# Input loaded group by group among the weights, shorter stores and loads of the far sets, and the heads' first stacks issued ahead of their tables

## The chip, the cores and the metric

The program runs on one core of a Trainium2 chip. The metric is the device time of one execution in microseconds (us). The core has five engines that run their own instruction streams: PE (TensorE; "PEld" are its weight loads), DVE (VectorE), ACT (ScalarE), POOL (GpSimd) and SP (SyncE, which here only issues DMAs). DMAs are moved by 16 shared DMA engines.

## What is computed

The reference is a network of eight residual stages on x of 4 x 1024 x 256 in float32. The change touches the first stage and the start of the program:

```python
x = x + _L0_attn_a_ref(_layernorm(x, axis=-1), W_q, W_k, W_v, W_o, W_down_kv, W_up_k, W_up_v)

# _L0_attn_a_ref, with 16 heads of 16
q = x @ W_q
latent_kv = (x @ W_k + x @ W_v) @ W_down_kv      # 64 wide
k_rec, v_rec = latent_kv @ W_up_k, latent_kv @ W_up_v
scores = einsum('bhqd,bhkd->bhqk', q, k_rec) / sqrt(256)
scores = scores * exp(-0.01 * |i - j|)
attn = softmax(scores); out = attn @ v_rec; return out @ W_o
```

Seven further stages follow (a mixture of experts, a retention, the experts again, a windowed attention, a low-rank FFN, a gated recurrence, the FFN again). The change does not touch their code.

## The kernel before

X, the residual stream, stays in SBUF as one tile of 128 partitions x 32 tiles of tokens x 256. A group is four of these tiles, 512 tokens; there are NG = 8 groups, two to each of the 4 batches (h = 0 and h = 1). `network` opens a first block in which SP loads `ident` (64 KB), groups 0 and 1 of X (1 MB) and the other six (3 MB), and waits for the first two. The other engines wait at the end of that block. Then stage A (`attention_decay`) runs in three phases, each with a barrier behind it.

**Projection** (`project_latent`, names `s0Ap_`). SP starts with `ph.start`, which adds a constant to each of the phase's 19 counting semaphores, loads six weights and then two tables (`falls`, `grows`, each one row of decay repeated on 128 partitions, 512 KB). DVE waits for all six weights (line 1586), adds WkT and WvT, makes the LayerNorm of group 0, copies out the product with W_down_kv (`wlat`, line 1590), and makes the LayerNorm of group 1. PE waits for all weights too, forms `wlat`'s product (line 1639), and only then transposes group 0 (line 132). From there each group g passes through the same turn: PE multiplies the latent (L1649) and q (L1656), transposes group g + 1, and multiplies k (L1665) and v (L1671); DVE multiplies each of q and k by both tables, which gives four sets F (0: q by falls, 1: q by grows, 2: k by grows, 3: k by falls; L1602); ACT rounds each set to its top part (L1500), and DVE (sets 0 and 1, L1505) or POOL (sets 2 and 3, L1511) forms the rest. SP stores top and rest of each set to the DRAM tensor `parts`: 64 stores of 512 KB in all, 8 to a group, in rows of 2 KB.

**Heads** (`heads_decay`, names `s0Ah_`). Two heads make a pair, and a pair has 16 turns (8 key tiles x 2 heads). SP loads for each pair two stacks, `plus` (sets 0 and 2) and `minus` (sets 1 and 3, the far side of the diagonal), each by 8 DMAs. At the phase's start SP issues in this order: `table` and `seen`, the first plus stack, then, once POOL has written `ones`, twelve DMAs of `ones` into rows of the six k tiles, and then the second plus, first minus and third plus stacks. PE waits for the twelve and for a zeroed PSUM bank before anything else, then computes 30 score turns ahead (`score`, two matmuls of 128 x 512 each, L2055), of which DVE takes the maximum (L2000) with the help of `table`, out of two PSUM buffers. Then the main loop runs: next to each further score turn PE forms the shifted scores (L2080), a transposed diagonal tile (L2089) and, after ACT's exponential (L2024), the product with V (L2100). The rows of `ones` are read from L2080 on. The minus stack is only multiplied where the key tile lies after the query tile, so key tile 0 and query tile 7 of it are never read.

**Output** (`project_heads`, names `s0Ao_`) follows; it does not change.

The lines that matter most:

```python
pe.wait_ge(weights, loaded)            # projection, PE and DVE: all six weights
pe.wait_ge(oned, 16 * 12)              # heads, PE, before the first score
```

## Time and profile before

| | us |
|---|---|
| median of 3 runs | 3270.99 (3268.53 to 3271.00) |
| the profiled execution | 3270.93 |
| its span, first to last record | 3269.2 |
| until the first matmul of the groups (L1649) | 27.6 |
| last bytes of `parts` stored | 134 |
| first matmul of the heads (L2055) | 150.4 |
| first matmul of their main loop (L2080) | 188.8 |

Over the span PE is busy for 86%, DVE for 60%, ACT for 48%, POOL for 31%. The page's slices show PE nearly full in the heads and in most later stages, and idle or light in the first 150 us. The granted TensorE clock has two levels, 1.2 GHz (0.50 in the rows) and 2.4 GHz (1.00). A row of the timeline gives start, busy time, engine, line, what is written from what, and in brackets how long the engine sat idle before it and what ended that.

### The profile page before, as it was taken

To read this page: it belongs to the slowest core of one execution; us is meant where nothing else is said; L and a number is where in the kernel's file an instruction comes from. 1 tells how busy PE (TensorE), PEld (TensorE's weight loads), DVE (VectorE), ACT (ScalarE), POOL (GpSimd) and SP (SyncE) were. 2 spreads that over 40 slices of the span, in tenths; PEclk is the share of its full clock that TensorE was granted. 3 is DMA by queue.
4 is the path that set the end of the run, shared out by engine and by line. 5 is a ranking of instruction groups with operands and counts; after the bars stand their busy time and mean duration, and the time that the engine had idled before them with its cause. 6 is when DMAs were issued, how large, how long until landed. Compare 5 with 4: busy or idle time off the path is not lost. (4 is left out here: it accounts for less than half of the span.)

```text
span 3269.2 us, 48231 instructions
## 1 busy us (share of the span) xinstructions
PE 2802.9 (86%) x15883; PEld 1690.3 (52%) x15883; DVE 1958.6 (60%) x4266; ACT 1558.7 (48%) x2949; POOL 1004.0 (31%) x1384
## 2 busy tenths in 40 slices
PE   6599999999986299997883499996969997888879
PEld 3244444444443198985551498983534443534443
DVE  6578878888826744443558644444956663527852
ACT  3347777777751145453111345442326665245544
POOL 3322222222201145452001245442664442120112
PEclk9779999999998599998996699997979998898879
DMA  7813232323224144432003244423243442200001
GB/s 254 282 46 83 66 86 67 85 67 80 62 70 134 45 91 86 95 71 65 0 0 130 65 96 84 98 38 89 79 123 96 101 99 66 56 1 0 0 7 46
DMA packets 183271, 253.89 MB, mean 78 GB/s; under 512 B 39416, under 2 KB 124152, under 8 KB 183056
## 3 DMA queue, kind: packets, MB, share of 16 engines
q1 hardware_dynamic: 151616, 216.89, 22.3%
q0 software_dynamic: 30720, 33.98, 6.5%
q8 instruction: 113, 1.85, 0.2%
q14 instruction: 102, 0.84, 0.1%
q10 hardware_dynamic: 720, 0.33, 0.1%
HBM read 156.53 MB, written 93.00 MB: 76 GB/s over the span
## 5 line engine op out<-in xcount | busy, mean ns | idle before, releaser
L2000 DVE CUSTOM_DVE_ANT_0 s0Ah_SD<-s0Ah_ps_s,s0Ah_table 128x1024 f32<-128x1024 f32 x512 | 607.1, 1223 | 157.1 <-PE s0Ah_ps_s L2055 157.1
L2024 ACT ACTIVATE s0Ah_PM<-s0Ah_ps_x 128x512 f32<-128x512 f32 x1024 | 530.1, 601 | 188.0 <-PE s0Ah_ps_x L2080 98.1
L2055 PE MATMUL s0Ah_ps_s<-s0Ah_plus_k,s0Ah_plus_q 48*128 48x512 f32 x1024 | 422.9, 477 | 31.9 <-DMA s0Ah_minus_k<-s0Ah_ones 28.0
L1980 POOL TENSOR_TENSOR s0Ah_DG<-s0Ah_SD,s0Ah_mx 128x128 f32<-128x128 f32 x512 | 205.5, 401 | 554.0 <-DVE s0Ah_mx L2000 554.0
L2055 PEld LDWEIGHTS s0Ah_ps_s<-s0Ah_plus_k,s0Ah_plus_q 48*128 48x128 f32 x1024 | 167.4, 193 | 279.6 <-DVE s0Ah_mx L2000 176.7
L2100 PE MATMUL s0Ah_ps_v<-s0Ah_PM,s0A_V 128*17 128x512 f32 x2048 | 271.9, 603 | 0.0
L2080 PE MATMUL s0Ah_ps_x<-s0Ah_plus_q,s0Ah_plus_k 50*128 50x512 f32 (+3 forms) x640 | 238.0, 389 | 0.0
L2260 DVE CUSTOM_DVE_ANT_0 s4Ch_SD<-s4Ch_ps_s,s4Ch_table 128x264 f32<-128x264 f32 x448 | 177.4, 431 | 94.6 <-PE s4Ch_ps_s L2345 90.1
L2080 PE MATMUL s0Ah_ps_x<-s0Ah_minus_q,s0Ah_minus_k 50*128 50x512 f32 (+3 forms) x640 | 218.9, 390 | 0.0
L2289 ACT ACTIVATE s4Ch_PM<-s4Ch_ps_x 128x512 f32<-128x512 f32 (+1 forms) x256 | 131.4, 564 | 113.7 <-PE s4Ch_ps_x L2372 110.5
L2089 PE MATMUL s0Ah_ps_x<-top_ident,s0Ah_DG 128*128 128x128 f32 x512 | 169.0, 330 | 0.0
L1288 ACT ACTIVATE s1Me_hid<-s1Me_ps_h 128x512 f32<-128x512 f32 x128 | 76.7, 599 | 183.1 <-PE s1Me_ps_h L1326 183.1
L1288 ACT ACTIVATE s3Me_hid<-s3Me_ps_h 128x512 f32<-128x512 f32 x128 | 76.7, 599 | 182.8 <-PE s3Me_ps_h L1326 182.8
L1189 POOL DMA_INDIRECT s1M_acc<-s1Me_ys,s1Me_keep x64 | 111.2, 1738 | 166.0 <-DVE s1Me_ys L1253 151.4
L1189 POOL DMA_INDIRECT s3M_acc<-s3Me_ys,s3Me_keep x64 | 109.6, 1712 | 163.8 <-DVE s3Me_ys L1253 149.2
L1243 DVE TENSOR_TENSOR s1Me_HT_rest<-s1Me_hid,s1Me_HT_top 128x512 fp32r<-128x512 f32 x128 | 89.0, 695 | 102.7 <-ACT s1Me_HT_top L1289 98.5
L1243 DVE TENSOR_TENSOR s3Me_HT_rest<-s3Me_hid,s3Me_HT_top 128x512 fp32r<-128x512 f32 x128 | 89.0, 695 | 102.5 <-ACT s3Me_HT_top L1289 99.0
L1340 PE MATMUL s1Me_ps_o<-s1Me_w_top,s1Me_HT_top 128*128 128x256 f32 x512 | 145.0, 283 | 0.0
L1340 PE MATMUL s3Me_ps_o<-s3Me_w_top,s3Me_HT_top 128*128 128x256 f32 x512 | 145.0, 283 | 0.0
L1340 PE MATMUL s3Me_ps_o<-s3Me_w_rest,s3Me_HT_top 128*128 128x256 f32 x512 | 144.0, 281 | 0.0
L1340 PE MATMUL s1Me_ps_o<-s1Me_w_rest,s1Me_HT_top 128*128 128x256 f32 x512 | 144.0, 281 | 0.0
L1340 PE MATMUL s1Me_ps_o<-s1Me_w_top,s1Me_HT_rest 128*128 128x256 f32 x512 | 143.8, 281 | 0.0
(438 smaller groups left out, 6736.3 us busy)
## 6 DMA issues: line engine op xcount, KB each, us to landing
...
s1W_raw_w<-in_L_ffn_w SPq DMA_DIRECT2D x16, 1024.0 KB
s3W_raw_w<-in_L_ffn_w SPq DMA_DIRECT2D x16, 1024.0 KB
...
```

Source lines behind the costliest of these rows:

```text
L1189: pool.indirect_dma_start(out=acc[:, :], out_offset=bass.IndirectOffsetOnAxis(ap=keep[:, BH * v + k // C, k % C:k % C + 1], axis=0), in_=y ...
L1243: nc.vector.tensor_tensor(HT[1][:, m, :], hid[:, m % NH, :], HT[0][:, m, :].bitcast(F32), ALU.subtract).then_inc(h_rest, 1)
L1288: nc.scalar.activation(hid[:, m % NH, :], ps_h[:, m % NH, :], ACT.Gelu_apprx_tanh)
L1340: x = nc.tensor.matmul(ps_o[:, k // 2, (k % 2) * D:(k % 2 + 1) * D], HT[hp][:, m, k * P:(k + 1) * P], w2p[s][wp][:, m, :], start=(m == 0 a ...
L1980: nc.gpsimd.tensor_tensor(DG[p % 3][:, r * TB + t, :], SD[i % NSD][:, t * P:(t + 1) * P], mx[p % 3][:, r * TB + t:r * TB + t + 1].to_broad ...
L2000: nc.vector.tensor_tensor_reduce(SD[i % NSD][:, :], ps_s[i % 2][:, :, :].rearrange("p a n -> p (a n)"), table[:, (TB - 1 - t) * P:(TB - 1 ...
L2024: nc.scalar.activation(PM[n % NPB][:, :], ps_x[u % NX][:, :], ACT.Exp).then_inc(e_ok, 1)
L2055: x = nc.tensor.matmul(ps_s[i % 2][:, half, :], q[at(r), t * P:(t + 1) * P], k[at(r), half * GT:(half + 1) * GT], start=True, stop=True)
L2080: x = nc.tensor.matmul(bank[:, lo:hi], k[with_m(r), t * P:(t + 1) * P], q[with_m(r), half * GT + lo:half * GT + hi], start=True, stop=True)
L2089: nc.tensor.transpose(ps_x[u % NX][:, t % G * P:(t % G + 1) * P], DG[p % 3][:, r * TB + t, :], ident[:, :]).then_inc(x_mm, 1)
L2100: x = nc.tensor.matmul(ps_v[j * 32:j * 32 + HD + 1, :], V[:, n // H, n % H, t, :], PM[w % NPB][:, :], start=(t == 0), stop=(t == TB - 1), ...
L2260: nc.vector.tensor_tensor_reduce(SD[i % NS][:, 0:n], ps_s[i % NS][:, 0:n], mask, 1.0, -3e38, ALU.add, ALU.max, accum_out=mx[p % 3][:, r * ...
```

## The change

Three edits, all in stage A and ahead of it.

1. The first block is gone, with its semaphores and their release at the program's end. SP now loads X in the projection itself, in eight DMAs of one group each, with a semaphore for each: group 0, `ident`, the three weights of the latent (WkT, WvT, W_down_kv, on a semaphore of their own), group 1, the other three weights, the two tables, groups 2 to 7. DVE begins with the LayerNorm of group 0 and adds WkT and WvT behind it; PE begins with the transposes of group 0 and forms `wlat`'s product behind them. DVE waits for group g + 2 at the start of turn g.
2. Sets 1 and 3 are stored without the tile that is never read: in the groups with h = 1 set 1 loses its last 128 columns, in those with h = 0 set 3 its first. The stores of these sets that are cut have rows of 1.5 KB. The minus stacks are loaded without them, 896 columns wide.
3. In the heads, `table` and `seen` are issued by ACT, and so are the twelve DMAs of `ones`, behind ACT's square of the table. SP starts with the first plus stack and goes on with the next stacks at once. PE waits for `ones` and the zeroed bank behind its 30 score turns.

```diff
-        loaded, rest = top.sem("loaded"), top.sem("rest")
-        with nc.Block() as block:
...
-                sp.dma_start(ident[:, :], a["ident"]).then_inc(loaded, 16)
-                sp.dma_start(X[:, 0:2 * G, :], x[:, 0:2 * G, :]).then_inc(loaded, 16)
-                sp.dma_start(X[:, 2 * G:, :], x[:, 2 * G:, :]).then_inc(rest, 16)
-                sp.wait_ge(loaded, 32)
...
         @block.sync
         def _(sp):
             ph.start(sp)
+            for g in range(2):
+                sp.dma_start(X[:, g * G:(g + 1) * G, :], x[:, g * G:(g + 1) * G, :]).then_inc(x_in[g], 16)
+                if g == 0:
+                    sp.dma_start(ident[:, :], a["ident"]).then_inc(ident_in, 16)
+                    load_once(sp, latent, latent_in)
             load_once(sp, weights, pairs)
             load_once(sp, tabled, [(falls[:, :], a["decay"][0:1, T - P:].to_broadcast([P, T])),
                                    (grows[:, :], a["decay"][P - 1:P, 0:T].to_broadcast([P, T]))])
+            for g in range(2, NG):
+                sp.dma_start(X[:, g * G:(g + 1) * G, :], x[:, g * G:(g + 1) * G, :]).then_inc(x_in[g], 16)
...
         def _(dve):
-            dve.wait_ge(weights, loaded)
+            dve.wait_ge(x_in[0], 16)
+            ln.vector(dve, 0)
+            dve.wait_ge(latent, 16 * len(latent_in))
             nc.vector.tensor_tensor(wkT[:, :, :], wkT[:, :, :], wvT[:, :, :], ALU.add).then_inc(consts, 1)
-            ln.vector(dve, 0)
...
+                    dve.wait_ge(x_in[g + 2], 16)
                     ln.vector_moments(dve, g + 2)
...
         def _(pe):
-            pe.wait_ge(weights, loaded)
+            pe.wait_ge(ident_in, 16)
+            ln.tensor(pe, 0)
+            pe.wait_ge(latent, 16 * len(latent_in))
             pe.wait_ge(consts, START + 1)
...
             pe.wait_ge(consts, START + 2)
-            ln.tensor(pe, 0)
+            pe.wait_ge(weights, 16 * len(pairs))
...
+        def cols(k):
+            return slice(P if k == 3 and h == 0 else 0, GT - P if k == 1 and h == 1 else GT)
...
+                qs, ks = (slice(0, T - P), slice(P, T)) if which else (slice(0, T), slice(0, T))
...
             load(0, 0, plus[0], plus_in[0])
-            sp.wait_ge(ones_ok, START + 1)
-            for _, k in plus + minus:
-                for r in range(2):
-                    sp.dma_start(k[r * 64 + SROW:r * 64 + MROW, :].bitcast(F32), ones[:, :]).then_inc(oned, 16)
             load(1, 0, plus[1], plus_in[1])
...
+            act.dma_start(table[:, T - P:], a["decay"][:, T - P:]).then_inc(tabled, 16)
+            act.dma_start(seen[:, :], a["masks"][:, 0:P]).then_inc(tabled, 16)
             act.wait_ge(tabled, 32)
             nc.scalar.activation(table[:, T - P:], table[:, T - P:], ACT.Square, scale=D ** 0.5).then_inc(table_ok, 1)
+            act.wait_ge(ones_ok, START + 1)
+            for _, k in plus + minus:
+                for r in range(2):
+                    act.dma_start(k[r * 64 + SROW:r * 64 + MROW, :].bitcast(F32), ones[:, :]).then_inc(oned, 16)
...
-            pe.wait_ge(oned, 16 * 12)
-            pe.wait_ge(zero_ok, START + 1)
...
                 if i == U + 2:
                     turned(0)
+            pe.wait_ge(oned, 16 * 12)
+            pe.wait_ge(zero_ok, START + 1)
```

Three places show the new order. The first is the issue order of SP at the start of the program (`in_` are inputs in DRAM). Before:

```order
L2582 DMA top_ident<-in_ident 128x128
L2583 DMA top_X<-in_L_attn_a_x 128x8x256
L2584 DMA top_X<-in_L_attn_a_x 128x24x256
L2578 UNCONDITIONAL_BRANCH [waits top_loaded]
L1561 UNCONDITIONAL_BRANCH [waits barrier_Pool_Activation_PE_DVE_SP_release]
L146 DMA s0Ap_wkT<-in_WkT 128x2x256
L146 DMA s0Ap_wvT<-in_WvT_a 128x2x256
L146 DMA s0Ap_wq<-in_L_attn_a_W_q 128x2x256
L146 DMA s0Ap_wd<-in_L_attn_a_W_down_kv 128x2x64
```

And now:

```order
L1567 UNCONDITIONAL_BRANCH [waits barrier_Pool_Activation_PE_DVE_SP_release]
L1571 DMA top_X<-in_L_attn_a_x 128x4x256
L1573 DMA top_ident<-in_ident 128x128
L146 DMA s0Ap_wkT<-in_WkT 128x2x256
L146 DMA s0Ap_wvT<-in_WvT_a 128x2x256
L146 DMA s0Ap_wd<-in_L_attn_a_W_down_kv 128x2x64
L1571 DMA top_X<-in_L_attn_a_x 128x4x256
L146 DMA s0Ap_wq<-in_L_attn_a_W_q 128x2x256
L146 DMA s0Ap_wuk<-in_L_attn_a_W_up_k 64x256
L146 DMA s0Ap_wuv<-in_L_attn_a_W_up_v 64x256
L146 DMA s0Ap_falls<-in_decay 128x1024
L146 DMA s0Ap_grows<-in_decay 128x1024
```

One group of X and the latent's weights now lead, and the last six groups stand behind everything. The second place is PE at the start of the projection, before:

```order
L1639 MATMUL s0Ap_ps_q<-s0Ap_wd,s0Ap_wkT 128x64 [waits s0Ap_consts,s0Ap_weights]
L1639 MATMUL s0Ap_ps_q<-s0Ap_wd,s0Ap_wkT 128x64 x3
L132 MATMUL s0Ap_ps_t<-top_ident,s0Ap_ln_h 128x128 [waits s0Ap_ln_hT,s0Ap_ln_hrow,s0Ap_consts]
L132 MATMUL s0Ap_ps_t<-top_ident,s0Ap_ln_h 128x128 x7
L1649 MATMUL s0Ap_ps_l<-s0Ap_hT,s0Ap_wlat 64x512 [waits s0Ap_l_ok,s0Ap_ln_hT]
```

And now:

```order
L132 MATMUL s0Ap_ps_t<-top_ident,s0Ap_ln_h 128x128 [waits s0Ap_ln_hT,s0Ap_ln_hrow,s0Ap_ident_in]
L132 MATMUL s0Ap_ps_t<-top_ident,s0Ap_ln_h 128x128 x7
L1656 MATMUL s0Ap_ps_q<-s0Ap_wd,s0Ap_wkT 128x64 [waits s0Ap_consts,s0Ap_latent]
L1656 MATMUL s0Ap_ps_q<-s0Ap_wd,s0Ap_wkT 128x64 x3
L1666 MATMUL s0Ap_ps_l<-s0Ap_hT,s0Ap_wlat 64x512 [waits s0Ap_ln_hT,s0Ap_l_ok,s0Ap_weights,s0Ap_consts]
```

The transposes and the latent's product have changed places, and the wait for all weights stands at the first matmul of the groups. The third place is SP at the start of the heads, before:

```order
L1914 DMA s0Ah_table<-in_decay 128x1024
L1915 DMA s0Ah_seen<-in_masks 128x128
L1922 DMA s0Ah_plus_q<-s0A_parts 32x1024
...
L1927 DMA s0Ah_plus_k<-s0A_parts 16x1024
L1949 DMA s0Ah_plus_k<-s0Ah_ones 2x1024 x8
L1949 DMA s0Ah_minus_k<-s0Ah_ones 2x1024 x4
L1922 DMA s0Ah_plus_q<-s0A_parts 32x1024
```

On ACT the same DMAs now stand around the square of the table:

```order
L2044 DMA s0Ah_table<-in_decay 128x1024
L2045 DMA s0Ah_seen<-in_masks 128x128
L2047 ACTIVATE s0Ah_table<-s0Ah_table 128x1024
L2051 DMA s0Ah_plus_k<-s0Ah_ones 2x1024 x8
L2051 DMA s0Ah_minus_k<-s0Ah_ones 2x1024 x4
```

Fourteen DMAs have left SP's queue there: two ahead of the first stack, twelve behind it.

## Rows read from the trace of the kernel before

**Rows 1.** Timeline of the program's start: start, busy, engine, line, operation, [idle before <- releaser].

```profile
0.76 0.39 SPq L2582 DMA_DIRECT2D top_ident<-in_ident  x1
1.21 0.41 SPq L2583 DMA_DIRECT2D top_X<-in_L_attn_a_x  x1
...
8.43 1.56 SPq L146 DMA_DIRECT2D s0Ap_wkT<-in_WkT  x1
...
19.39 0.69 DVE L1587 TENSOR_TENSOR s0Ap_wkT<-s0Ap_wkT,s0Ap_wvT 128x512 f32<-128x512 f32 x1 [19.39 <-DMA s0Ap_wuv<-in_L_attn_a_W_up_v]
...
20.23 1.94 PE L1639 MATMUL s0Ap_ps_q<-s0Ap_wd,s0Ap_wkT 128*128 128x64 f32 x8 [20.23 <-DVE s0Ap_wkT L1587]
...
23.28 1.38 DVE L115 TENSOR_SCALAR s0Ap_ln_h<-top_X,s0Ap_ln_mv,s0Ap_ln_rstd 128x256 f32<-128x256 f32 x4 [1.42 <-POOL s0Ap_ln_rstd L125]
24.58 0.28 DVE L1590 COPY s0Ap_wlat<-s0Ap_ps_q 128x128 f32<-128x128 f32 x1
...
24.92 1.97 PE L132 MATMUL s0Ap_ps_t<-top_ident,s0Ap_ln_h 128*128 128x128 f32 x8 [2.74 <-DVE s0Ap_wlat L1590]
...
27.56 3.67 PE L1649 MATMUL s0Ap_ps_l<-s0Ap_hT,s0Ap_wlat 128*64 128x512 f32 x4 [0.67 <-ACT s0Ap_hT L140]
```

**Rows 2.** DMA issues of stage A: count, KB each, median us from issue to landing.

```profile
top_X<-in_L_attn_a_x SPq DMA_DIRECT2D x1, 3072.0 KB, 14.3
...
s0Ah_plus_k<-s0A_parts SPq DMA_DIRECT2D x18, 64.0 KB, 2.9
...
top_X<-in_L_attn_a_x SPq DMA_DIRECT2D x1, 1024.0 KB, 5.7
...
top_ident<-in_ident SPq DMA_DIRECT2D x1, 64.0 KB, 1.8
```

**Rows 3.** Timeline of the groups' turns: two turns of PE and POOL's last work.

```profile
40.48 1.93 PE L1649 MATMUL s0Ap_ps_l<-s0Ap_hT,s0Ap_wlat 128*64 128x512 f32 x4
...
51.50 1.93 PE L1649 MATMUL s0Ap_ps_l<-s0Ap_hT,s0Ap_wlat 128*64 128x512 f32 x4
...
124.09 4.64 POOL L1511 TENSOR_TENSOR s0Ap_sp_rest<-s0Ap_sp_F,s0Ap_sp_top 128x1024 fp32r<-128x1024 f32 x2 [7.63 <-ACT s0Ap_sp_top L1500]
```

**Rows 4.** Windows: PE, PEld, DVE, ACT, POOL busy, granted clock, DMA share, GB/s.

```profile
100.00:102.00 2.00, 2.00 (x5) 0.68 (x4) 2.00 (x2) 1.99 (x3) 1.35 (x1) 1.00 0.32 109
...
102.00:134.00 32.00, 18.25 (x50) 7.97 (x48) 14.08 (x13) 12.04 (x19) 14.19 (x6) 0.79 1.02 376
...
134.00:135.00 1.00, 0.00 (x0) 0.00 (x0) 0.00 (x0) 0.00 (x0) 0.00 (x0) 0.50 0.05 18
```

**Rows 5.** Timeline of the heads' start, to the first score and maximum.

```profile
136.37 0.35 SPq L1914 DMA_DIRECT2D s0Ah_table<-in_decay  x1
...
137.24 0.43 SPq L1922 DMA_DIRECT2D s0Ah_plus_q<-s0A_parts  x1
...
140.77 1.06 ACT L2032 ACTIVATE s0Ah_table<-s0Ah_table 128x1024 f32<-128x1024 f32 x1 [15.81 <-DMA s0Ah_seen<-in_masks]
141.02 0.58 SPq L1927 DMA_DIRECT2D s0Ah_plus_k<-s0A_parts  x1
...
146.70 2.38 SPq L1949 DMA_DIRECT2D s0Ah_minus_k<-s0Ah_ones  x4
...
150.41 1.22 PE L2055 MATMUL s0Ah_ps_s<-s0Ah_plus_k,s0Ah_plus_q 48*128 48x512 f32 x4 [28.03 <-DMA s0Ah_minus_k<-s0Ah_ones]
...
151.67 1.23 DVE L2000 CUSTOM_DVE_ANT_0 s0Ah_SD<-s0Ah_ps_s,s0Ah_table 128x1024 f32<-128x1024 f32 x1 [9.51 <-PE s0Ah_ps_s L2055]
```

**Rows 6.** Timeline of PE in the score turns and in the main loop.

```profile
155.50 2.36 PE L2055 MATMUL s0Ah_ps_s<-s0Ah_plus_k,s0Ah_plus_q 48*128 48x512 f32 x4 [0.18 <-DVE s0Ah_mx L2000]
...
188.78 0.66 PE L2080 MATMUL s0Ah_ps_x<-s0Ah_plus_q,s0Ah_plus_k 50*128 50x384 f32 x1
...
206.23 1.91 PE L2100 MATMUL s0Ah_ps_v<-s0Ah_PM,s0A_V 128*17 128x512 f32 x8
...
210.34 1.05 PE L2100 MATMUL s0Ah_ps_v<-s0Ah_PM,s0A_V 128*17 128x512 f32 x8
```

More of the change, by code:

```diff
@@ L1435, with attention_decay @@
 KBLK = NGL + P
-def attention_decay(nc, ph, X, ident, a, rest):
+def attention_decay(nc, ph, X, ident, a):
     parts = nc.dram_tensor(f"{ph.name}_parts", (SETS, B * D, 2, T), F32, kind="Internal").ap()
@@ L1445, in attention_decay @@
         with ExitStack() as first:
-            project_latent(nc, Phase(nc, first, ph.name + "p"), X, ident, a, parts, V, rest)
+            project_latent(nc, Phase(nc, first, ph.name + "p"), X, ident, a, parts, V)
         heads_decay(nc, Phase(nc, own, ph.name + "h"), ident, a, parts, V, (OD, OS))
@@ L1515, in sync @@
         s, b, h = g % 2, g // 2, g % 2
-        to = lambda k, part: self.parts[k, b * D:(b + 1) * D, part, h * GT:(h + 1) * GT].rearrange(
-            "(c p) t -> p c t", p=P)
+        def cols(k):
+            return slice(P if k == 3 and h == 0 else 0, GT - P if k == 1 and h == 1 else GT)
+        to = lambda k, part: self.parts[k, b * D:(b + 1) * D, part, h * GT + cols(k).start:h * GT + cols(k).stop
+                                        ].rearrange("(c p) t -> p c t", p=P)
         for k in range(self.n):
             sp.wait_ge(self.top_ok, START + g * self.n + k + 1)
-            sp.dma_start(to(k, 0), self.top[s][k][:, :, :].bitcast(F32)).then_inc(self.written[s], 16)
+            sp.dma_start(to(k, 0), self.top[s][k][:, :, cols(k)].bitcast(F32)).then_inc(self.written[s], 16)
             if k < self.by_dve:
@@ L1529, in all_written, with project_latent @@
             sp.wait_ge(self.written[s], 16 * 2 * self.n * (NG // 2))
-def project_latent(nc, ph, X, ident, a, parts, V, rest):
+def project_latent(nc, ph, X, ident, a, parts, V):
     DL = a["L0_attn_a_W_down_kv"].shape[1]
@@ L1549, in project_latent @@
     split = SplitSets(ph, parts, SETS, 2)
-    weights, tabled = ph.dma_sem("weights"), ph.dma_sem("tabled")
+    latent, weights, tabled = ph.dma_sem("latent"), ph.dma_sem("weights"), ph.dma_sem("tabled")
+    ident_in = ph.dma_sem("ident_in")
+    x_in = [ph.dma_sem(f"x_in{g}") for g in range(NG)]
     consts, wl_mm, table_ok = ph.sem("consts"), ph.sem("wl_mm"), ph.sem("table_ok")
@@ L1554, in project_latent @@
     part = lambda w: w.rearrange("(c p) n -> p c n", p=P)
[L1555 to L1556 removed]
+    latent_in = [(wkT[:, :, :], part(a["WkT"])), (wvT[:, :, :], part(a["WvT_a"])),
+                 (wd[:, :, :], part(a["L0_attn_a_W_down_kv"]))]
+    pairs = [(wq[:, :, :], part(a["L0_attn_a_W_q"])), (wuk[:, :], a["L0_attn_a_W_up_k"]),
              (wuv[:, :], a["L0_attn_a_W_up_v"])]
[L1558 removed]
+    x = a["L0_attn_a_x"].rearrange("b (j p) d -> p (b j) d", p=P)
     with nc.Block() as block:
@@ L1591, in _ @@
                                   ).then_inc(consts, 1)
+            dve.wait_ge(x_in[1], 16)
             ln.vector(dve, 1)
-            dve.wait_ge(rest, 16)
             dve.wait_ge(table_ok, START + 2)
@@ L1913, in _ @@
             ph.start(sp)
-            sp.dma_start(table[:, T - P:], a["decay"][:, T - P:]).then_inc(tabled, 16)
-            sp.dma_start(seen[:, :], a["masks"][:, 0:P]).then_inc(tabled, 16)
             def load(p, which, tiles, done):
+                qs, ks = (slice(0, T - P), slice(P, T)) if which else (slice(0, T), slice(0, T))
+                n = T - P if which else T
                 for r in range(2):
@@ L1921, in load @@
                     z = r * 64
-                    sp.dma_start(q[z:z + 2 * HD, :], parts[which, rows, :, :].rearrange("d n t -> (d n) t")
+                    sp.dma_start(q[z:z + 2 * HD, qs], parts[which, rows, :, qs].rearrange("d n t -> (d n) t")
                                  ).then_inc(done, 16)
-                    sp.dma_start(q[z + 2 * HD:z + 3 * HD, :], parts[which, rows, 0, :]).then_inc(done, 16)
-                    sp.dma_start(k[z:z + 2 * HD, :], parts[2 + which, rows, 0:1, :].to_broadcast([HD, 2, T])
+                    sp.dma_start(q[z + 2 * HD:z + 3 * HD, qs], parts[which, rows, 0, qs]).then_inc(done, 16)
+                    sp.dma_start(k[z:z + 2 * HD, ks], parts[2 + which, rows, 0:1, ks].to_broadcast([HD, 2, n])
                                  ).then_inc(done, 16)
-                    sp.dma_start(k[z + 2 * HD:z + 3 * HD, :], parts[2 + which, rows, 1, :]).then_inc(done, 16)
+                    sp.dma_start(k[z + 2 * HD:z + 3 * HD, ks], parts[2 + which, rows, 1, ks]).then_inc(done, 16)
             def maxima(p):
@@ L2596, in network @@
                 if stage == "A":
-                    attention_decay(nc, ph, X, ident, a, rest)
+                    attention_decay(nc, ph, X, ident, a)
                 if stage == "M":
```

8 lines of the change are left out of this document (1 added, 7 removed).

## The prediction

> **What bounds the kernel now.** I read the page's slices first, then the timeline of each place that the diff touches. The slices put PE near full from 190 us on, and the heads' main loop is one unbroken row of matmuls; an edit that ends before it is worth what it moves that loop's start, 188.78 us [rows 6], and nothing that follows can hide or give back such a shift, since all later stages run behind barriers. So the question is what sets 188.78, and it has four links.
>
> (a) Until 19.39 us nothing computes. DVE and PE wait for six weights, which SP issued from 8.43 us on, behind 3 MB of X that took 14.3 us to land [rows 1, 2]. From there a serial chain of add, LayerNorm, product and transposes leads to the groups' first matmul at 27.56 us [rows 1].
>
> (b) The eight turns. PE's period is 51.50 - 40.48 = 11.02 us where the clock stays at 1.00 [rows 3]. One group's stores are 8 x 524,288 bytes = 4.19 MB, at 376 GB/s [rows 4] 11.15 us. Compute and DMA are nearly tied. The turns end on POOL at 124.09 + 4.64 = 128.73 us [rows 3], while the DMA engines are full from 102 us on and still carry a backlog until 134 us [rows 4].
>
> (c) After the barrier PE starts the heads at 150.41 us, and what ended its wait is the last `ones` DMA, not the stack it multiplies [rows 5].
>
> (d) In the 30 score turns PE waits 0.18 us for DVE before each pair even at the low clock [rows 6], so DVE paces them: 188.78 - 150.41 = 38.4 us. The change alters nothing in that pace.
>
> **First block and X by groups.** SP's first DMA went out at 0.76 us [rows 1]. Now `ph.start` stands ahead of it. Between the landing of X's first part, 1.21 + 5.7 = 6.9 us, and the first weight at 8.43 us lie 1.5 us with a barrier in them [rows 1, 2], so `ph.start` costs 0 to 1.5 us; I take 1.1 and an issue at 1.9 us. Landing: 64 KB took 1.8 us, 1 MB behind it 5.7 us after an issue 0.45 us later, that is 6.15 us for 1088 KB [rows 1, 2]; on that line 512 KB take 1.8 + 448/1024 x 4.35 = 3.7 us. Group 0 lands at 5.6; I take 5.8 for `ident` and the weights that share the engines. The latent's three weights (576 KB) are issued within about 3 us behind it and land by 9 us.
>
> Then the same work in the new order. From the first moments to the end of the rows h: before 20.08 (19.39 + 0.69) to 24.66 (23.28 + 1.38) = 4.6 us, now to 10.4. PE's transposes 0.26 + 1.97, to 12.6; DVE's add lies beside them. The product of the latent 1.94, to 14.6. The copy of `wlat` 0.28 and its two handovers, to 15.1 [rows 1]. The groups' first matmul then starts at about 15.3, before 27.56: **-12.2 us**. The other three weights (384 KB) must have landed by then: with all that stands ahead they are 2.1 MB, at 376 GB/s [rows 4] 5.5 us behind a start at about 3. Bounds: a landing 1.7 us later gives -10.5; a landing 0.8 us earlier, together with half of the 3.67 us of L1649 at the higher clock, gives -14.
>
> The new waits for groups 2 to 7 stand on DVE ahead of the turn's moments, with all four F behind them, and PE and ACT wait for those. Up to group 2 3.7 MB must move, 10 us at that rate, so about 13 us; turn 0 asks for it near 21. Group 7 needs 2.6 MB more and lands near 20, before the first store near 25, so the loads cost the stores nothing. The tables land near 12; ACT's scaling ends before its first latent copy. These are hidden, and would cost at most the difference of those times if not.
>
> The order on SP no longer has the block's wait and barrier; the removed semaphores also take one release and barrier from the program's end. Nothing in my rows isolates its price; a whole boundary between phases is 136.37 - 134 = 2.4 us from last bytes to SP's next issue [rows 4, 5], and this is a part of one without a DMA wait. Between 0 and 1.5 I take **-0.4**.
>
> **Far sets.** Each group stores two DMAs of 384 instead of 512 columns, 0.26 MB less or 0.7 us, 5.6 us for eight. Most of that is lost: the DMA engines idle more, since the turns' period is 11.02 and the stores now need 10.45. What counts is the backlog behind the last pause, at 100 to 102 us, where the share was 0.32 [rows 4]. After it come the stores of nearly three groups: 3 x 0.7 = **-2.0 us** at the end, 134 becomes 132. The floor is POOL's end at 128.73 plus issue, 1.4 us of transfer and about 1 us of landing, 131.3, so -2.7 at most; if the shorter rows move no faster, each packet costing the same, 0. I take -2.0: X has rows of 1 KB, and its last 3 MB landed 14.3 + 0.45 - 5.7 = 9.05 us behind its first (the issues lie as far apart as the two before them) [rows 1, 2], 348 GB/s against 376 with rows of 2 KB, so rows of 1.5 KB should lose some 4%, 0.1 us of the 2.
>
> In the heads the minus stacks are 1/8 smaller. No matmul waits for them (the main loop starts 30 us after their issue), so 0.
>
> **Heads' start.** SP's first issue takes the table's place, 136.37. The first stack's last DMA started 141.02, now 141.02 - (137.24 - 136.37) = 140.15 [rows 5]; 2.9 us to landing [rows 2] gives 143.05. I add 0.45 for the table's 590 KB, which now flow beside the stack: PE starts at 143.5 instead of 150.41, **-6.9 us**. Bounds: the full 1.6 us of the table's bytes at 376 GB/s give -5.7, none -7.4.
>
> The Trainium skill, "DMA: Bandwidth & Descriptors", section "Issuing engines are not separate DMA queues", says that DMAs started by ScalarE run on the same 16 engines and interleave with the others, so only the issue time is saved. By it the table would slow the stack by up to its whole transfer, and this term would be -5.7; no row here shows two queues at once.
>
> Does DVE find its table? Its square started 4.4 us after the issue [rows 5]; with 1.6 us added it ends at 143.5, and the first maximum, 1.26 us behind PE, is at 144.7. It holds by about 1 us. ACT then issues twelve DMAs at 0.6 us each (2.38 / 4 [rows 5]), 7.2 us to 151; ACT's next work was due only after 18 score turns, near 168, and PE asks for `ones` after 30, near 182. Covered. SP's next stack goes out 8 us earlier, and PE needs it after 16 turns.
>
> **The sum.** -12.2 - 2.0 - 6.9 - 0.4 = -21.5 us. The profiled execution took 3270.93 (span 3269.2), the median is 3270.99, so they are the same: **3249.4 us**. With all terms at one end -25.7 (bounds -14, -2.7, -7.4, -1.5), at the other -16.2.
>
> **Rivals.**
> 1. The clock in the main loop rises at another point. It started at 188.78 at the low clock, and the same 8 matmuls took 1.91 us at 206.23 and 1.05 at 210.34 [rows 6]: some 20.4 us ran at 1.2 GHz, where work takes 1.82 times as long, so these cost 9.2 us. PE's idle time before the heads shrinks from 28 to about 19 us, which can help. If the rise comes at once, 3240; halfway, 3245. If it comes 10 us later, +4.5, 3254, or 20 later, 3258. For it: in this trace the rise came late with PE full, so it hangs on something. Against: the instructions from the first score on are the same at the same distances.
> 2. One large term fails: the table or the stack lands late, or the groups' first matmul waits for a load that comes out of its turn. Losing 6 to 9 us gives 3255 to 3259. For it: the stack, the table and the next stack compete at once. Against: the bytes.
> 3. The turns are bound by the stores, not by PE, so the early start only fills a queue. Then 134 moves by the DMA work alone. But the stores start with the first turn too, so they move with it; only if both loads and stores fought would it be near 3262 to 3268. Little speaks for it.
> 4. Slower: after the earlier scores the clock stays low much longer. At 0.45 us lost per us, it must stay low 48 us longer to eat the 21.5, and 62 us to be slower by 0.2%: then 3277.5 or more. The trace shows 85 us at 0.50 between 124 and 209 us but 20 of them with a full PE.
>
> **Chances.** The sum 0.62 (own range 3245 to 3255); rival 1 earlier 0.13, later 0.08; rival 2 0.08; rival 3 0.04; rival 4 0.02; beyond 0.03. The range 3240 to 3258 holds the sum, both sides of the clock and most of rival 2, some 0.85 by count, and I keep it for what I overlooked. A measurement can tell about 0.2%, 6.5 us, from no change: faster 0.94, same 0.04, slower 0.02.
>
> **What would show it.** In the changed profile: group 0 landing before 6.5 us; L1666 starting at 15.3 (14 to 17); the same 11 us turns; stores ending near 119.8, with more pauses in the DMA row; PE's first score 9.5 us behind that, released by the plus stack; the first L2080 near 167.3; and a rise of the clock about 20 us behind it. From there every stage should lie 21 us earlier. If DVE's first maximum names ACT's table as releaser, or if L1617 waits for an x_in, the cover that I named is gone.

## The result, and the profile after

The changed kernel takes 3248.68 us (median of 4 runs, 3244.14 to 3253.19), the kernel before beside it 3270.99 us (4 runs, 3268.53 to 3273.92). The ratio is 0.9932, 95% interval 0.9920 to 0.9944, that is 18 to 26 us faster. The forecast was 3249.4 us. The profiled execution took 3250.33 us with a span of 3248.6 us; the span before was 3269.2 us. All runs of this document but one lie within 0.9% of the fastest run of the same kernel, at a mean granted clock of 0.907 to 0.917; the one, of the kernel with the table behind the stack, took 3528.03 us at 0.769 and is left out of that kernel's time.

I read the start first. The timeline of the changed kernel (start, busy, engine, line, operation, idle before and its releaser), to be held against [rows 1]:

```profile
1.89 0.44 SPq L1571 DMA_DIRECT2D top_X<-in_L_attn_a_x  x1
...
6.21 1.41 DVE L106 BATCH_NORM_STATS2 s0Ap_ln_st<-top_X 128x6 f32<-128x256 f32 x4 [6.21 <-DMA top_X<-in_L_attn_a_x]
...
9.49 1.38 DVE L115 TENSOR_SCALAR s0Ap_ln_h<-top_X,s0Ap_ln_mv,s0Ap_ln_rstd 128x256 f32<-128x256 f32 x4 [1.42 <-POOL s0Ap_ln_rstd L125]
...
10.97 1.94 PE L132 MATMUL s0Ap_ps_t<-top_ident,s0Ap_ln_h 128*128 128x128 f32 x8 [10.97 <-DVE s0Ap_ln_h L115]
12.70 1.81 PE L1656 MATMUL s0Ap_ps_q<-s0Ap_wd,s0Ap_wkT 128*128 128x64 f32 x8
14.55 0.29 DVE L1604 COPY s0Ap_wlat<-s0Ap_ps_q 128x128 f32<-128x128 f32 x1 [3.08 <-PE s0Ap_ps_q L1656]
14.89 3.67 PE L1666 MATMUL s0Ap_ps_l<-s0Ap_hT,s0Ap_wlat 128*64 128x512 f32 x4 [0.38 <-DVE s0Ap_wlat L1604]
...
111.47 4.64 POOL L1511 TENSOR_TENSOR s0Ap_sp_rest<-s0Ap_sp_F,s0Ap_sp_top 128x1024 fp32r<-128x1024 f32 x2 [5.97 <-ACT s0Ap_sp_top L1500]
```

`ph.start` let the first issue go at 1.89 us. The first work on DVE was released by X at 6.21 us, not by weights at 19.39 as in [rows 1]. The groups' first matmul starts at 14.89 instead of 27.56 us, 12.7 us earlier, and no wait for a load stands between. POOL's last work ends at 111.47 + 4.64 = 116.11 instead of 128.73 us [rows 3], 12.6 us earlier: the eight turns kept their pace.

Then the stores. Windows (PE, PEld, DVE, ACT, POOL busy, granted clock, DMA share, GB/s), as in [rows 4]:

```profile
76.00:78.00 2.00, 2.00 (x5) 0.62 (x4) 2.00 (x3) 2.00 (x4) 0.98 (x1) 1.00 0.10 35
...
88.00:90.00 2.00, 2.00 (x3) 0.50 (x2) 1.61 (x2) 1.31 (x2) 1.96 (x1) 0.50 0.75 272
...
100.00:102.00 2.00, 2.00 (x5) 0.68 (x4) 0.99 (x1) 2.00 (x3) 1.30 (x1) 1.00 0.64 237
...
102.00:120.00 18.00, 6.39 (x18) 2.85 (x16) 6.89 (x6) 5.22 (x9) 8.14 (x4) 0.74 1.02 374
...
120.00:121.00 1.00, 0.00 (x0) 0.00 (x0) 0.00 (x0) 0.00 (x0) 0.00 (x0) 0.50 0.39 143
```

The DMA engines pause in every turn up to 102 us, are full from there on, and the last bytes move near 120.4 us, where it was 134.05 [rows 4]. The page's line on DMA gives 248.64 MB now and 253.89 MB before, 5.25 MB less.

The heads' start, against [rows 5]:

```profile
122.06 0.39 ACTq L2044 DMA_DIRECT2D s0Ah_table<-in_decay  x1
...
122.70 0.34 SPq L1939 DMA_DIRECT2D s0Ah_plus_q<-s0A_parts  x1
...
126.39 0.58 SPq L1944 DMA_DIRECT2D s0Ah_plus_k<-s0A_parts  x1
127.01 0.42 SPq L1939 DMA_DIRECT2D s0Ah_plus_q<-s0A_parts  x1
...
127.50 5.42 ACTq L2051 DMA_DIRECT2D s0Ah_plus_k<-s0Ah_ones  x8
...
131.33 1.23 PE L2071 MATMUL s0Ah_ps_s<-s0Ah_plus_k,s0Ah_plus_q 48*128 48x512 f32 x4 [21.56 <-DMA s0Ah_plus_k<-s0A_parts]
...
132.58 1.23 DVE L2013 CUSTOM_DVE_ANT_0 s0Ah_SD<-s0Ah_ps_s,s0Ah_table 128x1024 f32<-128x1024 f32 x1 [3.71 <-PE s0Ah_ps_s L2071]
```

PE is now released by the plus stack, as intended, at 131.33 instead of 150.41 us. DVE's first maximum names PE, so the table was there in time. But the stack's last DMA, issued at 126.39, had landed only 4.9 us later.

Last the main loop, against [rows 6]:

```profile
169.81 0.65 PE L2096 MATMUL s0Ah_ps_x<-s0Ah_plus_q,s0Ah_plus_k 50*128 50x384 f32 x1
...
197.13 1.91 PE L2116 MATMUL s0Ah_ps_v<-s0Ah_PM,s0A_V 128*17 128x512 f32 x8
...
200.96 1.05 PE L2116 MATMUL s0Ah_ps_v<-s0Ah_PM,s0A_V 128*17 128x512 f32 x8
```

It starts 19.0 us earlier than before. The clock rises at 199.2 us, 29.4 us behind that start, where it had been 20.2 us in the profile before.

The table follows both profiles through the program, with what the difference grew or shrank by in each stretch.

| place | before, us | after, us | difference | step |
|---|---|---|---|---|
| groups' first matmul | 27.56 | 14.89 | -12.7 | -12.7 |
| POOL's last work of the turns ends | 128.73 | 116.11 | -12.6 | +0.1 |
| SP's first DMA of the heads | 136.37 | 122.70 | -13.7 | -1.1 |
| first score | 150.41 | 131.33 | -19.1 | -5.4 |
| main loop starts | 188.78 | 169.81 | -19.0 | +0.1 |
| last product with V starts | 950.6 | 935.4 | -15.2 | +3.8 |
| s5F's last product starts | 2935.9 | 2919.3 | -16.6 | -1.4 |
| s7F's last product starts | 3263.3 | 3243.2 | -20.1 | -3.5 |
| span | 3269.2 | 3248.6 | -20.6 | -0.5 |

The end release is visible in SP's waits of the last microseconds (waiting, what for: us, times, longest), before and then after:

```profile
SPq L62 <- PEq L62: 1.2, 3, 0.6
```

```profile
SPq L62 <- PEq L62: 0.8, 2, 0.4
```

One barrier less, 0.4 us.

Three steps of the table are not in the change's code at all: +3.8 us in the main loop, -1.4 us in the stages up to s5F (the low-rank FFN), and -3.5 us in the last two stages, which are the gated recurrence and an FFN. The first and the last nearly cancel. So the experiments had to answer two questions: do the three edits bring what their terms say, and where do these other steps come from?

### The profile page after: what moved, and what is told of

Read it like the earlier page. It is cut to its first block and busy times, and to the rows that moved or that the text cites. A ratio compares the mean times of both kernels' runs of the same rounds, so it can differ in the third digit from the quotient of the medians.

```text
span 3248.6 us, 48213 instructions
## 1 busy us (share of the span) xinstructions
PE 2803.9 (86%) x15883; PEld 1690.6 (52%) x15883; DVE 1958.3 (60%) x4266; ACT 1558.0 (48%) x2949; POOL 1002.2 (31%) x1384
## 2 busy tenths in 40 slices
DMA packets 183367, 248.64 MB, mean 77 GB/s; under 512 B 39512, under 2 KB 128344, under 8 KB 183152
## 3 DMA queue, kind: packets, MB, share of 16 engines
q10 hardware_dynamic: 1056, 1.02, 0.1%
## 5 line engine op out<-in xcount | busy, mean ns | idle before, releaser
L2307 ACT ACTIVATE s4Ch_PM<-s4Ch_ps_x 128x512 f32<-128x512 f32 (+1 forms) x256 | 131.3, 564 | 114.0 <-PE s4Ch_ps_x L2390 110.7
```

## The three edits alone, and the change again

**Edit 1 alone** (X by groups, no first block; edits 2 and 3 left out).

```diff
-                sp.dma_start(X[:, 0:2 * G, :], x[:, 0:2 * G, :]).then_inc(loaded, 16)
-                sp.dma_start(X[:, 2 * G:, :], x[:, 2 * G:, :]).then_inc(rest, 16)
...
+            for g in range(2):
+                sp.dma_start(X[:, g * G:(g + 1) * G, :], x[:, g * G:(g + 1) * G, :]).then_inc(x_in[g], 16)
```

> Edit 1 alone (no first block, X by groups); far sets and the heads' start as before. Theory A (the terms of the sum add): the groups' first matmul at 14.9 us as in the changed kernel, the whole schedule up to the heads' first score 12.7 us earlier (first score near 137.7), about 13 us in the end: 3258. Rival B (the stores bind the turns, an early start only fills their queue): first score at 141 or later, gain under 10 us.

Measured: 3258.58 us against 3271.96, ratio 0.9957 (0.9945 to 0.9970). The timeline:

```profile
15.10 3.18 PE L1663 MATMUL s0Ap_ps_l<-s0Ap_hT,s0Ap_wlat 128*64 128x512 f32 x4 [0.38 <-DVE s0Ap_wlat L1601]
...
123.66 0.35 SPq L1928 DMA_DIRECT2D s0Ah_table<-in_decay  x1
...
137.67 1.22 PE L2069 MATMUL s0Ah_ps_s<-s0Ah_plus_k,s0Ah_plus_q 48*128 48x512 f32 x4 [28.21 <-DMA s0Ah_minus_k<-s0Ah_ones]
...
176.03 0.65 PE L2094 MATMUL s0Ah_ps_x<-s0Ah_plus_q,s0Ah_plus_k 50*128 50x384 f32 x1
```

The first matmul moves by 12.5 us, SP's first DMA of the heads by 12.7, the first score by 12.7, the main loop by 12.75. With full stores the early start reaches the heads undiminished. That refutes the rival by which the stores bind the turns and an early start only fills their queue.

**Edit 2 alone** (the unused tile of sets 1 and 3).

```diff
-            sp.dma_start(to(k, 0), self.top[s][k][:, :, :].bitcast(F32)).then_inc(self.written[s], 16)
+            sp.dma_start(to(k, 0), self.top[s][k][:, :, cols(k)].bitcast(F32)).then_inc(self.written[s], 16)
```

> Edit 2 alone (short stores and loads of the far sets). Theory A: the turns are paced by TensorE, so of the 5.6 us that the stores save only the backlog's share shows, 1 to 2 us at the end of the stores (132 to 133 instead of 134), ratio 0.9995. Rival B (the stores bind the turns): up to 5 us earlier, first score at 145 to 146.

Measured: 3271.23 us, ratio 1.0002 (0.9993 to 1.0011). The timeline:

```profile
124.91 4.65 POOL L1511 TENSOR_TENSOR s0Ap_sp_rest<-s0Ap_sp_F,s0Ap_sp_top 128x1024 fp32r<-128x1024 f32 x2 [7.63 <-ACT s0Ap_sp_top L1500]
...
135.93 0.35 SPq L1917 DMA_DIRECT2D s0Ah_table<-in_decay  x1
```

From POOL's end to SP's first DMA it takes 135.93 - 129.56 = 6.4 us here and 136.37 - 128.73 = 7.6 us before: the smaller backlog gives 1.3 us. But in this trace the turns themselves ended 0.8 us later, from a first matmul at 28.08, and the first score lies at 150.37, as before. A gain of a microsecond is there in one stretch and cannot be measured in the time.

**Edit 3 alone** (heads' start).

```diff
-            sp.dma_start(table[:, T - P:], a["decay"][:, T - P:]).then_inc(tabled, 16)
-            sp.dma_start(seen[:, :], a["masks"][:, 0:P]).then_inc(tabled, 16)
...
+            act.dma_start(table[:, T - P:], a["decay"][:, T - P:]).then_inc(tabled, 16)
+            act.dma_start(seen[:, :], a["masks"][:, 0:P]).then_inc(tabled, 16)
```

> Edit 3 alone (the heads' first stacks ahead, tables and ones on ScalarE's queue). Theory A as the changed kernel showed it: the first score comes 8.6 us behind SP's first DMA of the heads instead of 14.0, a gain of 5.4 us before the score turns, first score at 145.0 and about 5 us in the end. My prediction's own number was 6.9 (first score at 143.5). Rival B (the clock in the main loop rises later because the heads start in another phase of it): the main loop starts 5 us earlier but the end gains under 2 us.

Measured: 3265.66 us, ratio 0.9987 (0.9978 to 0.9996).

```profile
136.44 0.34 SPq L1920 DMA_DIRECT2D s0Ah_plus_q<-s0A_parts  x1
...
145.71 1.22 PE L2052 MATMUL s0Ah_ps_s<-s0Ah_plus_k,s0Ah_plus_q 48*128 48x512 f32 x4 [23.36 <-DMA s0Ah_plus_k<-s0A_parts]
```

9.3 us from SP's first DMA to the first score, where it was 14.0 before: -4.8 us, less than the forecast's bound of -5.7.

**The changed kernel again.**

> The changed kernel once more, unchanged. In its first trace TensorE's clock rose 29.3 us behind the first shifted score, in the kernel before 20.4. If that point depends on the code alone it is again 29 us; if it varies from execution to execution (rival C: this is what spreads its times over 9 us), this trace has another distance, and the time goes with it at 0.45 us per us.

Measured: 3253.01 us (10 runs, 3243.09 to 3272.3) against 3271.96 (27 runs), ratio 0.9945 (0.9929 to 0.9961), or -19.0 us. The three edits alone gave -13.4, -0.7 and -6.3 us by their medians, together -20.4, between the -22.3 of the first comparison and the -19.0 of this one. By the ratios they gave -14.1, +0.7 and -4.3 us, together -17.7, beside -18.0 for all three. The terms add, as far as times can tell that scatter by several us; edit 2 cannot be told from nothing.

## What holds the stack back

Three things can hold back the first stack's last DMA: the table on ACT's queue, the next stacks behind it on SP's, and the `ones` that ACT issues from 127.50 us on. The profile counts each queue's packets (queue: packets, MB, share of the 16 engines; q1 is SP's, q10 is ACT's, which carried 0.33 MB in all before the change and 1.02 MB now). In the changed kernel from 122.5 to 125.0 us, from 125.0 to 131.3 us, and from 127.5 to 131.3 us:

```profile
q10 hardware_dynamic: 157, 0.53, 69.2%
```

```profile
q1 hardware_dynamic: 471, 1.19, 102.2%
```

```profile
q10 hardware_dynamic: 4, 0.01, 1.2%
```

SP had issued the stack from 122.70 us on, but until 125.0 only packets of ACT's queue moved: the table did not flow beside the stack, it went ahead of it. Behind 125.0 the engines are full with the stack and the next ones. The `ones` put 0.01 MB into the last 3.8 us, too little to hold anything back. A full engine does not mean the rate of the stores, 374 GB/s, either:

```profile
127.00:129.00 2.00, 0.00 (x0) 0.00 (x0) 0.29 (x1) 1.06 (x1) 0.00 (x0) 0.50 1.06 184
```

Two kernels tell the table's part from that of the next stacks.

**The table behind the stack**, issued by SP.

```diff
@@ sync, behind the first stack's last DMA
+            sp.dma_start(table[:, T - P:], a["decay"][:, T - P:]).then_inc(tabled, 16)
+            sp.dma_start(seen[:, :], a["masks"][:, 0:P]).then_inc(tabled, 16)
@@ scalar
-            act.dma_start(table[:, T - P:], a["decay"][:, T - P:]).then_inc(tabled, 16)
-            act.dma_start(seen[:, :], a["masks"][:, 0:P]).then_inc(tabled, 16)
```

> The changed kernel with table and seen issued by SP behind the first stack instead of by ScalarE beside it. In the changed kernel the first stack's last DMA was issued at 126.39 us and its landing released the first score only at 131.33, 4.9 us later, where I had counted 2.9 + 0.45. Theory A (the table's 590 KB on the second queue slow the stack): now the first score starts at 129.3 to 129.8, but the table comes late and VectorE's first maximum is at 132.8 or later, so no gain in time. Rival B (the next stacks, issued right behind, or the stack's own slow reads cost the 2 us): the first score stays at 131.

Measured: 3246.19 us (3 runs) against 3268.44, ratio 0.9936 (0.9912 to 0.9960), not to be told from the changed kernel.

```profile
125.62 0.58 SPq L1944 DMA_DIRECT2D s0Ah_plus_k<-s0A_parts  x1
126.24 0.42 SPq L1963 DMA_DIRECT2D s0Ah_table<-in_decay  x1
...
128.69 1.23 PE L2071 MATMUL s0Ah_ps_s<-s0Ah_plus_k,s0Ah_plus_q 48*128 48x512 f32 x4 [19.68 <-DMA s0Ah_plus_k<-s0A_parts]
...
130.38 1.06 ACT L2047 ACTIVATE s0Ah_table<-s0Ah_table 128x1024 f32<-128x1024 f32 x1 [18.80 <-DMA s0Ah_seen<-in_masks]
...
131.89 1.22 DVE L2015 CUSTOM_DVE_ANT_0 s0Ah_SD<-s0Ah_ps_s,s0Ah_table 128x1024 f32<-128x1024 f32 x1
```

From 122.0 to 124.5 us SP's queue now moves at once, and the engines have room:

```profile
q1 hardware_dynamic: 95, 0.26, 42.1%
```

The stack lands 128.69 - 125.62 = 3.1 us behind its last issue (2.8 in a second trace), close to the 2.9 us of [rows 2], against 4.9 with the table ahead of it. The `ones` go later too in this kernel, since ACT issues them behind the table's square at 130.38, but the packets above leave them no weight. But now DVE waits for the table. Its first maximum comes 131.89 - 121.92 = 10.0 us behind SP's first issue; in the changed kernel that is 132.58 - 122.70 = 9.9. What the stack wins, the table loses.

**The next stacks held** until the first has landed; the table stays on ACT's queue.

```diff
             load(0, 0, plus[0], plus_in[0])
+            sp.wait_ge(plus_in[0], LOADS)
             load(1, 0, plus[1], plus_in[1])
```

> The changed kernel, where SP waits for the first stack's landing before it issues the next ones. Theory A (the table slows the first stack): the first score stays at 131.0 to 131.4. Rival B (the next stacks slow it): first score at 129.3 to 130, about 1.5 us in the end if all else is the same.

Measured: 3249.84 us, ratio 0.9942 (0.9923 to 0.9960).

```profile
122.58 0.34 SPq L1939 DMA_DIRECT2D s0Ah_plus_q<-s0A_parts  x1
...
126.27 0.58 SPq L1944 DMA_DIRECT2D s0Ah_plus_k<-s0A_parts  x1
130.23 0.30 SPq L1939 DMA_DIRECT2D s0Ah_plus_q<-s0A_parts  x1
130.26 1.23 PE L2072 MATMUL s0Ah_ps_s<-s0Ah_plus_k,s0Ah_plus_q 48*128 48x512 f32 x4 [20.47 <-DMA s0Ah_plus_k<-s0A_parts]
...
131.51 1.23 DVE L2014 CUSTOM_DVE_ANT_0 s0Ah_SD<-s0Ah_ps_s,s0Ah_table 128x1024 f32<-128x1024 f32 x1 [3.23 <-PE s0Ah_ps_s L2072]
```

Now 4.0 us from the last issue, and the first maximum 131.51 - 122.58 = 8.9 us behind SP's first. The changed kernel has 4.9 and 9.9 in its first trace, 4.6 and 9.5 in its second. So of the 2.0 us beyond 2.9, the next stacks are 0.6 to 1 when the table goes first, and the table the rest. Holding them is worth 0.6 to 1 us at this place by single traces, below what the time can show.

The rule that the prediction weighed (the Trainium skill, "DMA: Bandwidth & Descriptors", section "Issuing engines are not separate DMA queues") holds here in what it says of the gain: moving the table to ACT's queue saved SP's issue time, not the table's transfer. Its word that DMAs of several engines interleave is not what these 2.5 us show, in which one queue's packets went and the other's waited.

## Can a busier TensorE bring the clock up earlier?

In every trace PE works at 0.50 through the score turns, with short waits for DVE, and on into the full main loop. One explanation of where the rise falls is how full PE's row is in the score turns. If so, matmuls whose result nobody reads, put into PE's waits, should bring the rise forward. Four kernels add such spare matmuls of `ident` to the changed kernel, into `ps_v`, which is free until the main loop; PE also waits ahead of the score turns until that bank is zeroed. Nothing else changes.

```diff
+            def spare():
+                for _ in range(1):
+                    nc.tensor.matmul(ps_v[0:HD + 1, 0:P], ident[:, 0:HD + 1], ident[:, :], start=True, stop=True)
...
+                if i >= 2:
+                    spare()
```

This is the first, with 28 of them. The second has two of them behind each of the last 12 score turns (`i >= 18`); the third one of full size (`ps_v[:, 0:P]`, `ident` by `ident`) behind the last 12; the fourth two of full size behind the last 8.

> The changed kernel with one spare matmul (ident by ident, 17 rows x 128 columns, into rows of ps_v that the first product with V overwrites) behind each of 28 of the 30 score turns. They take about 0.43 us each at 1.2 GHz, in time in which TensorE waits for VectorE. Theory C (the late rise of the clock, 31 us behind the main loop's start, costs 0.45 us per us, and a fuller TensorE in the score turns brings it ahead): the clock is at 2.4 GHz when the main loop starts, the heads end up to 14 us earlier, 3237 to 3242. Rival D (the rise hangs on something else): the rise stays 16 to 31 us behind the first L2096 matmul, and the time is the same or up to 3 us longer.

> The same with two spare matmuls behind each of the last 12 score turns alone. At 1.2 GHz they make a turn up to 0.45 us longer than VectorE's 1.27. Theory C: the clock rises within a few of these turns and the main loop starts at 2.4 GHz, gain 10 to 14 us less 1 to 3 us for the longer turns. Rival D: 2 to 5 us slower than the changed kernel.

> The changed kernel with one spare 128 x 128 matmul (ident by ident, all 128 rows and columns of the array, into the first 128 columns of ps_v before its first use) behind each of the last 12 score turns. The spare matmuls with only 17 output rows kept TensorE full for 50 us and the clock stayed at 1.2 GHz. Theory E (the small share of the array that scores and spares used, 48 input rows or 17 output rows, kept the clock low): it rises within these 12 turns or right behind, distance from the main loop's start to the rise under 5 us instead of 29.5, heads over 745 to 752 us from the main loop's start instead of 765.6, minus up to 5 us for longer score turns: 3238 to 3245. Rival D (it hangs on something else): distance 8 to 30 us as before, no gain beyond the spread, and up to 5 us lost in the score turns.

> The same with two such matmuls behind each of the last 8 score turns. Theory E: rise within or right behind the score turns, as above, 3238 to 3245. Rival D: distance 8 to 30 us, 3 to 7 us slower than the changed kernel from the longer turns.

| kernel | median, us | ratio (95%) | main loop starts | clock rises | distance |
|---|---|---|---|---|---|
| one narrow, 28 turns | 3262.03 | 0.9982 (0.9971 to 0.9993) | 181.41 | 202.2 | 20.8 |
| two narrow, 12 turns | 3258.24 | 0.9969 (0.9957 to 0.9980) | 179.65 | 188.5 | 8.85 |
| one full, 12 turns | 3255.65 | 0.9949 (0.9934 to 0.9964) | 176.63 | 206.0 | 29.4 |
| two full, 8 turns | 3258.88 | 0.9962 (0.9948 to 0.9976) | 178.75 | 214.0 | 35.3 |

The windows of the first of them, and its spare matmuls (count, shortest, median and longest in ns):

```profile
130.00:168.00 38.00, 35.36 (x86) 13.33 (x86) 26.32 (x43) 0.42 (x2) 8.81 (x22) 0.50 0.33 58
168.00:200.00 32.00, 32.00 (x101) 12.43 (x101) 20.14 (x33) 10.01 (x18) 6.81 (x17) 0.50 0.17 48
200.00:205.00 5.00, 5.00 (x30) 1.88 (x24) 2.71 (x7) 2.43 (x5) 1.21 (x3) 0.78 0.02 5
...
L2122 PE MATMUL s0Ah_ps_v<-top_ident x56: 394/406/418, 135.0 to 181.1; 128*17 128x128 f32 x56
```

PE was busy 67.4 of 70 us by the records, at 0.50 all the while. The spares did not raise the clock in the score turns in any of the four; they only lengthened the turns, which start the main loop 7 to 12 us later. Each spare shows as two records of 0.41 us, where the expectation had counted one of 0.43, and PE had been idle for only about 4 us of the changed kernel's score turns (busy 34.7 of 38.8 us), so most of them found no wait to fill. The distance of the rise came out anywhere from 8.85 to 35.3 us, in no order with the work added. Both forms of the theory had called for a rise within these turns or right behind, and none came: neither the fuller row nor the larger matmuls brought it. All four have longer medians than the changed kernel; for one full matmul behind 12 turns the ratio, 0.9949 against 0.9945, does not tell them apart.

## Does the rise belong to the kernel or to the execution?

Two kernels were profiled once more, without an edit: the kernel before, and the one with the table behind the stack, whose first trace had shown the earliest rise of all.

> The kernel before, once more, for the clock alone. Its first trace had the clock's rise 20.2 us behind the start of the heads' main loop (matmuls there at the low clock until 209.0 us), a main loop of 761.8 us, and 327.4 us from the last product of s5F to that of s7F. If the place of the rise belongs to the kernel's instructions, this trace shows 20.2 again, within a us, and 761.8. If it is set by something that differs between executions, the distance lies anywhere between the 8.7 and 35.3 us seen so far, and the main loop's length follows it at 0.43 us per us. The last stretch shows 327.4 in the first case, and 324 or 327.4 in the second. The span before the heads stays as it was in both: first matmul of the groups at 27.6, first score at 150.4.

> The changed kernel with table and seen issued by SP behind the first stack, once more, for the clock alone. Its first trace had the clock's rise 8.7 us behind the start of the main loop and a main loop of 756.7 us. If the place belongs to the kernel, 8.7 and 756.7 come again; if it differs between executions, the distance lies elsewhere, most likely nearer to the 20 to 30 us that most traces show, and the loop is 5 to 9 us longer. First score near 128.7 and main loop start near 169.1 in both cases.

Measured: 3270.29 us and 3254.52 us, one run each, with 3270.47 for the kernel before beside them. The last eight products at the low clock and the first eight at the high one, for the kernel before:

```profile
215.92 1.91 PE L2100 MATMUL s0Ah_ps_v<-s0Ah_PM,s0A_V 128*17 128x512 f32 x8
...
220.03 1.05 PE L2100 MATMUL s0Ah_ps_v<-s0Ah_PM,s0A_V 128*17 128x512 f32 x8
```

In [rows 6] the same pair stands at 206.23 and 210.34. The same instructions, from a main loop that starts at 188.57 instead of 188.78, got the high clock 10 us later. For the other kernel:

```profile
197.53 1.91 PE L2116 MATMUL s0Ah_ps_v<-s0Ah_PM,s0A_V 128*17 128x512 f32 x8
...
201.43 1.05 PE L2116 MATMUL s0Ah_ps_v<-s0Ah_PM,s0A_V 128*17 128x512 f32 x8
```

Its first trace had a granted clock of 1.00 from 178 us on. The place of the rise differs between executions of one kernel. All traces without spare matmuls together:

| trace | main loop starts | clock rises | distance, us | main loop's length (to its last product's start), us | last product of s5F to that of s7F, us |
|---|---|---|---|---|---|
| before | 188.78 | 209.0 | 20.2 | 761.8 | 327.4 |
| before, again | 188.57 | 218.8 | 30.2 | 765.9 | 324.0 |
| after | 169.81 | 199.2 | 29.4 | 765.6 | 323.9 |
| after, again | 169.20 | 199.0 | 29.8 | 765.7 | 327.4 |
| edit 1 alone | 176.03 | 205.5 | 29.5 | 765.6 | 327.2 |
| edit 2 alone | 188.76 | 213.5 | 24.7 | 763.6 | 326.2 |
| edit 3 alone | 184.19 | 198.2 | 14.0 | 759.0 | 324.1 |
| table behind the stack | 169.11 | 177.8 | 8.7 | 756.7 | 327.4 |
| the same, again | 170.23 | 199.8 | 29.6 | 765.7 | 327.3 |
| next stacks held | 168.74 | 189.5 | 20.8 | 761.9 | 324.0 |

The length of the main loop follows the distance. From 8.7 us to 29.6 us in two traces of one kernel it grows by 9.0 us, 0.43 us for each; that is the price the prediction had worked out as 0.45. And the last stretch takes 324 or 326 to 327 us, in both kernels, with no tie to the edit: the kernel before shows 327.4 and 324.0, the changed one 323.9 and 327.4. Windows of its first part, 15 to 20 us behind the start of s5F's last product, show the clock at another level at the same place of the work, first before and then after:

```profile
2950.90:2955.90 5.00, 5.00 (x11) 2.02 (x10) 0.97 (x2) 1.17 (x2) 0.00 (x0) 0.76 0.00 0
```

```profile
2934.30:2939.30 5.00, 5.00 (x13) 2.16 (x12) 2.49 (x5) 1.76 (x3) 0.00 (x0) 1.00 0.00 0
```

Over the whole stretch the mean granted clock is 0.86 where it takes 327.4 us and 0.87 where it takes 324.0, in each kernel's two traces alike. The -1.4 us in the stages up to s5F is of the same size as the difference of the two traces of the kernel before there, 1985.3 and 1984.2 us.

So the pair to compare is the kernel before, second trace, with the changed kernel, first trace: the rise at 30.2 and 29.4 us, the last stretch 324.0 and 323.9. Their spans are 3268.4 and 3248.6 us, 19.8 us apart, and the main loops start 18.8 us apart. With 0.4 of the end release 0.6 us is left, spread over the stages between; I know no cause for it.

What decides in a given execution where the rise falls is open: nothing that I varied set it. The changed kernel's own two traces agree, at 29.4 and 29.8 us, so the scatter is shown by the two other kernels, and these traces are too few to say that the edit has no part in it.

The clock is also most of what spreads the single times. In its 14 executions the changed kernel took from 3243.09 us at a mean granted clock of 0.916 to 3272.3 us at 0.907. Worked out as twice the missing share of the span, that is 545 and 608 us at 1.2 GHz; the 64 us more, at the 0.43 us of the main loop, are 27 of the 29 us between them. This is an estimate, as the clocks are given to 0.001, or 6.5 us. Over all 14 the time grows by 0.45 us for each us at the low clock.

## Why the prediction was right

The time was right within a microsecond, better than its steps. Step by step:

1. **First block and X by groups, -12.2.** Measured -12.7, and in the kernel with this edit alone -12.5. First issue 1.89 (1.9 forecast), group 0 in use at 6.21 (5.8), the rows h ended at 10.87 (10.4), the first matmul at 14.89 (15.3). The last step won back what the landing had lost: the product of the latent, 1.81 us, followed the transposes without a gap. The covers that were named held: L1666 names DVE's copy as its releaser, and the turns kept their pace.
2. **The pass through the stores, 0 lost.** Right. POOL's end moved by 12.6, and edit 1 alone moved the first score by 12.7.
3. **Far sets, -2.0.** Mis-sized. The stretch from POOL's end to SP's first DMA shrank by 1.05 us in the change and by 1.3 in the kernel with this edit alone. The step that failed is the count of "nearly three groups" behind the last pause. The rows before gave 102 to 134 us; but with less to store, the engines catch up once more. In the changed kernel the last pause is also at 100 to 102 us, in a program that runs 12.6 us earlier, and behind it stand only 18.4 us of bytes. At 10.45 us a group these are 1.8 groups, and 1.8 x 0.7 = 1.2 us lies between the two that were measured.
4. **Heads' start, -6.9.** Mis-sized, and outside its own bounds of -5.7 to -7.4: -5.4 in the change, -4.8 alone. Two of its steps failed. The table did not flow beside the stack for 0.45 us: its packets went first, and the stack landed 4.94 us behind its last issue instead of 3.07 with the table behind it. The pessimistic bound, 1.6 us for the table's bytes, which is also what the prediction had by the Trainium skill's rule, was nearer. And the next stacks, which the term took as free because PE needs them late, took 0.6 to 1 us of that while they shared the engines with the first. A cost was missing since I asked only who needs those transfers, not whom they delay. With the 2.0 us beyond 2.9 in place of 0.45 the term comes to -5.4, as measured.
5. **End release, -0.4.** As measured.
6. **The pace of the score turns**, untouched: 38.5 us in the change, 38.4 before. ACT's twelve issues stayed covered.
7. **"Every later stage 21 us earlier."** This failed in the profile: -15.2 us behind the main loop, -16.6 behind s5F, -20.1 at the end. By its own words the forecast's rival 1, a rise 10 us later for +4.5 us, is what this trace showed, at +3.8. That it did not show in the span is luck: a gain of 3.5 us in the last two stages stood against it. Its condition was also wrong: the rival made the place of the rise a result of the edit, and the argument against it ("the same instructions at the same distances") made it a property of the code. The kernel before itself shows it at 20.2 and at 30.2 us.

The steps add up, by their own measured sizes, to -12.7 + 0.1 - 1.1 - 5.4 + 0.1 - 0.4 = -19.4 us, close to the 19.8 us of the two traces with like clocks. The forecast of -21.5 was about 2 us too hopeful, in terms 3 and 4; its lower bound adds up to -25.6, not -25.7. The medians, -22.3 in the first comparison and -19.0 in the second, allow both.

No kernel of the study is faster than the changed one beyond what can be measured. Holding the next stacks would add 0.6 to 1 us by the timelines.
